# Last batch of a gated cross-attention layer with routed experts: tile loads issued one by one, and routing steps placed in other slots of the vector engine's program

## The reference, cut to what matters

```python
x = x + tanh(g_xattn) * xattn(layernorm(x), ctx, mask, Wq, bq, Wk, bk, Wv, bv, Wo, bo)  # 16 heads, causal
x = x + tanh(g_ffn)  * ffn(layernorm(x), W1, b1, W2, b2, Wr, br)                        # 8 experts

def ffn(x):
    pick = argmax(softmax(x @ Wr + br))            # one expert per token
    out = 0
    for i in range(8):
        xi = x * (pick == i)                       # rows of other tokens are zero
        out = out + (relu(xi @ W1[i] + b1[i]) @ W2[i] + b2[i])
    return out
```

## Time and profile before

| | us |
|---|---|
| median of 3 runs | 373.57 |
| lowest, highest run | 372.77, 375.61 |
| the profiled execution, own time | 377.75 |
| its span, first to last instruction | 376.0 |
| mean granted TensorE clock of the span | 0.986 of full speed |

### The profile page before, as it was taken

One profiled execution on the slowest core, in us unless ns is written; L12 is line 12 of the kernel. 1 busy time (PEld: TensorE's weight loads), 2 busy tenths in 40 slices (PEclk: granted clock), 3 DMA queues, 4 the chain that ended last, 5 costly groups with the idle time before them and its releaser, 6 DMA issues.

```text
span 376.0 us, 11155 instructions
## 1 busy us (share of the span) xinstructions
PE 352.0 (94%) x2825; PEld 283.4 (75%) x2825; DVE 272.5 (72%) x1278; ACT 256.2 (68%) x931; POOL 191.6 (51%) x369
## 2 busy tenths in 40 slices
PE   7999998999999999999999999999998966968992
PEld 5777777777877887787788777877785645858992
DVE  4789993889488858776785788497837786566762
ACT  3687794878688859866876787678755445645661
POOL 6155563476356733782477257636653450335554
PEclk9999999999999999999999999999999898999998
DMA  6997220002000300030003000300008505023320
GB/s 206 255 367 195 90 89 0 3 3 89 29 0 0 101 14 0 0 115 0 0 0 115 0 0 7 123 0 0 0 28 347 217 30 155 24 83 96 102 69 12
DMA packets 21562, 27.87 MB, mean 74 GB/s; under 512 B 3649, under 2 KB 16789, under 8 KB 21536
## 3 DMA queue, kind: packets, MB, share of 16 engines
q1 hardware_dynamic: 19776, 23.85, 20.0%
q0 software_dynamic: 1504, 3.16, 2.5%
q10 hardware_dynamic: 256, 0.56, 0.7%
HBM read 19.00 MB, written 9.01 MB: 74 GB/s over the span
## 4 chain that ended last, share of the span: by engine, by line
PE 80%; DVE 6%; issue 4%; DMA 3%; ACT 2%; POOL 2%; SPq 1%; another core or an unknown queue 1%; POOLq 0%; DVEq 0%; ACTq 0%
PE ps_kv L1221 15%; PE ps_o L1221 14%; PE ps_s L1221 13%; PE ps_t L1320 12%; PE ps_w L1221 10%; PE ps_q L1221 7%; PE ps_t L1221 6%; DMA tile_in<-sorted_rows 2%; DVE masked L787 1%; POOL out L503 1%; DVE prob_T L806 1%; ACT prob L561 1%; SPq L355 1%; DMA nat<-in_ctx 1%; PE ps_w L1352 1%
## 5 line engine op out<-in xcount | busy, mean ns | idle before, releaser
L432 POOL TENSOR_SCALAR prob<-prob,row_inv 128x128 f32<-128x128 f32 (+1 forms) x256 | 104.8, 430 | 131.2 <-DVE row_inv L800 131.0
L561 ACT ACTIVATE prob<-masked,neg_max 128x128 f32<-128x128 f32 (+1 forms) x256 | 113.4, 444 | 52.9 <-DVE neg_max L787 51.3
L787 DVE CUSTOM_DVE_ANT_0 masked<-ps_s,mask_now 128x128 f32<-128x128 f32 (+1 forms) x256 | 78.9, 353 | 57.3 <-PE ps_s L1221 54.8
L806 DVE COPY prob_T<-ps_t 128x384 f32<-128x384 f32 x128 | 67.3, 548 | 1.4 <-PE ps_t L1320 1.4
L1320 PE MATMUL ps_t<-ident,prob 128*128 128x128 f32 x384 | 57.2, 284 | 3.2 <-DVE prob_T L806 3.0
L1320 PEld LDWEIGHTS ps_t<-ident,prob 128*128 128x128 f32 x384 | 41.4, 142 | 24.8 <-issue 20.8
L1221 PE MATMUL ps_s<-k_T,q_T 64*128 64x128 f32 (+1 forms) x512 | 59.6, 351 | 0.0
L1221 PE MATMUL ps_o<-prob_T,v_nat 128*64 128x256 f32 (+1 forms) x512 | 56.4, 342 | 0.0
L561 ACT ACTIVATION_READ_ACCUMULATOR prob<-masked,neg_max 128x1 f32 x256 | 47.8, 187 | 0.0
L1221 PEld LDWEIGHTS ps_o<-prob_T,v_nat 128*64 128x64 f32 x512 | 31.4, 137 | 17.4 <-issue 3.0
L503 POOL DMA_INDIRECT out<-tile_out,tile_in x23 | 23.7, 1031 | 37.2 <-DVE tile_out L1170 23.3
(11 more groups left out here) (197 smaller groups left out, 546.5 us busy)
## 6 DMA issues: line engine op xcount, KB each, us to landing
ctx_buf<-in_ctx SPq DMA_DIRECT2D x8, 768.0 KB
sorted_rows<-pad_rows SPq DMA_DIRECT2D x8, 642.5 KB
tile_in<-sorted_rows SPq DMA_DIRECT2D x24, 128.5 KB
packs<-in_L_ffn_W SPq DMA_DIRECT2D x1, 2048.0 KB
packs<-in_L_ffn_W SPq DMA_DIRECT2D x8, 256.0 KB
nat<-in_ctx SPq DMA_DIRECT2D x8, 128.0 KB, 3.6
nat<-in_x SPq DMA_DIRECT2D x1, 768.0 KB, 6.5
w_in<-in_L_xattn_Wk SPq DMA_DIRECT2D x2, 256.0 KB, 4.5
```

Source lines behind the costliest of these rows:

```text
L432: g.tensor_scalar(prob[:, slot, lo:hi], prob[:, slot, lo:hi], row_inv[:, slot, t:t + 1], 1.0, ALU.mult, ALU.mult).then_inc(prob_ready, 1)
L561: s.activation(prob[:, slot, lo:hi], masked[:, slot % 2, lo:hi], ACT.Exp, bias=neg_max[:, slot, t:t + 1], scale=-1.0, accum_out=row_sum[:, ...
L787: v.tensor_tensor_reduce(out=masked[:, slot % 2, lo:hi], in0=ps_s[slot % 2][:, lo:hi], in1=mask_now[:, lo:hi], scale=-SCALE, scalar=FLOOR, ...
L806: v.tensor_copy(prob_T[:, slot % TSLOTS, :], ps_t[slot % 2][:, 0:W3]).then_inc(probT_kept, 1)
```

## The change

SP reads the place of each early tile just before it issues that tile's load; the waits for the padding and for the scattered rows stand between the first read and the first load. On DVE, in the last batch: the 16 steps of the second norm stand in slots 0 to 7 in place of 0 to 9; the empty rows in slot 10 in place of 23; rest in slot 16 in place of 29; the early table in slots 28 and 30 in place of 24 to 27. On PE the transposes of the normalised rows stand in step 2 ahead of the values, in place of the end of step 1, and `rest_product` directly behind them in place of step 4. On ACT rest's store stands in step 3 in place of 5, its broadcast load in step 4 in place of 6; the first five `early_w1` stay in steps 5 and 6.

```diff
             sp.wait_ge(early_table_ready, 1)
-            early_at = [sp.value_load(tile_row[0:1, k:k + 1], min_val=0, max_val=PADROW) for k in range(EARLY)]
-            sp.wait_ge(padded, 16 * (E + 1))
-            sp.wait_ge(scattered, 16 * (NT - QT))
             for k in range(EARLY):
-                sp.dma_start(tile_in[:, k], sorted_rows[bass.ds(early_at[k], P), :]).then_inc(tile_loaded[k], 16)
+                at = sp.value_load(tile_row[0:1, k:k + 1], min_val=0, max_val=PADROW)
+                if k == 0:
+                    sp.wait_ge(padded, 16 * (E + 1))
+                    sp.wait_ge(scattered, 16 * (NT - QT))
+                sp.dma_start(tile_in[:, k], sorted_rows[bass.ds(at, P), :]).then_inc(tile_loaded[k], 16)
...
                     keep_oT(b, 8 * b + j, j)
-                    if last and j == REST_AT + 1:
+                    if last and j == 3:
                         act.wait_ge(rest_ready, 1)
                         act.dma_start(rest_rows[:, :], rest[:, :]).then_inc(rest_stored, 16)
+                    if last and j == 4:
+                        act.wait_ge(rest_stored, 16)
+                        act.dma_start(rest_all[:, :, :], rest_rows.rearrange("e d -> (e d)").partition_broadcast(P)
+                                      ).then_inc(rest_loaded, 16)
+                    if last and j == 5:
                         act.wait_ge(early_table_ready, 1)
                         act.wait_ge(ld_ffn, 16 * (E + 2))
                         for tile in range(2):
                             early_w1(tile)
-                    if last and j == REST_AT + 2:
-                        act.wait_ge(rest_stored, 16)
-                        act.dma_start(rest_all[:, :, :], rest_rows.rearrange("e d -> (e d)").partition_broadcast(P)
-                                      ).then_inc(rest_loaded, 16)
+                    if last and j == 6:
                         for tile in range(2, 5):
                             early_w1(tile)
...
-                if here == 6 * REST_AT - 1:
+                if here == EMPTY_AT:
                     dve.wait_ge(empty_done, 1)
...
-                if here == 6 * REST_AT + 5:
+                if here == REST_AT:
                     dve.wait_ge(rest_done, 1)
...
-                        if j == REST_AT:
+                        if j == 2:
+                            norm_transposes(b - 1, b + 1)
                             rest_product()
                     values(p, j)
                     if last and j > 0:
                         last_projection(j - 1)
-                    if last and j == 1:
-                        norm_transposes(b - 1, b + 1)
...
-REST_AT = 4
-LAST_NORM = {0: (0,), 1: (1,), 2: (2, 3), 3: (4, 5), 4: (6, 7), 5: (8, 9), 6: (10, 11), 7: (12, 13), 8: (14,), 9: (15,)}
+EMPTY_AT, REST_AT = 10, 16
+LAST_NORM = {0: (0,), 1: (1, 2, 3), 2: (4, 5), 3: (6, 7), 4: (8, 9), 5: (10, 11), 6: (12, 13), 7: (14, 15)}
 LAST_CHOOSE = {17: (0, 1, 2, 3, 4, 5)}
 LAST_PLACE = {21: (0, 1), 22: (2, 3)}
-LAST_TABLE = {24: (0, 1), 25: (2, 3), 26: (4, 5), 27: (6, 7)}
+LAST_TABLE = {28: (0, 1, 2, 3), 30: (4, 5, 6, 7)}
```

## The result

The changed kernel takes 369.77 us (median of 9 runs, 369.55 to 371.34) against 374.28 us before (median of 9, 372.77 to 377.04): a ratio of 0.9886, interval 0.9854 to 0.9919. It is 4.5 us faster (3.0 to 5.5 by the interval); the forecast said 4.4 and a time of 369.2. Times after also lie closer together: 1.8 us from lowest to highest, against 4.3.

A forecast was written before the change was run, and what follows sets the result against it. PE is busiest (94%), but DVE was taken to bound the last batch's stretch. Filled idle time and earlier table and loads bring batch 7's transposes 4.5 us earlier, less a tenth: 373.57 - 4.4 = 369.2 us, range 367.0 to 372.4.

The forecast's parts named there:

- The sum: Whole change: batch 7's transposes 4.5 us earlier, a tenth lost, saving 4.4 us carried whole to the end.
- Step 6: Batch 7's transposes: PE's order and DVE's norm both arrive near 318.1, 4.5 us earlier than 322.62.
- Step 5: SP's early tile loads: first load at 305.6, 4.6 us earlier; only 0.5 to 2.5 reach PE.
- Step 2: Table in slots 28 and 30: table 1.3 us earlier, PE's 2.44 wait shrinks, about 2 us gap before pair 7's transposes.
- Step 4: ACT: pair 7's output copied at 310.3, not 312.86; rest's store and broadcast cost nothing.
- Step 1: Norm, empty and rest rows on DVE and PE: filled idle time brings pair 6's copies 1.8 us earlier, to 304.8.
- Rival B: PE's low clock after two waits goes, gaining another 1.5 to 2 us: 367.4 us; chance 0.12.
- Rival C: The low clock moves to the new gap at 303.3, costing some 8 us, 1.5 hidden: 375.7 us; chance 0.06.

The follow-up runs named there:

- moves-only run: The changed kernel with SP's old seven reads put back ahead of the first load; ratio to before 0.9896.
- after again: The changed kernel, unaltered, timed and profiled a second time; 370.5 us, ratio to before 0.9866.
- later weight copies: The changed kernel with the last three of DVE's seven weight copies behind batch 7's choice and late table; ratios to before 0.9843 and, run again, 0.9833.
- one-filler profile: The kernel before plus 20 identity transposes, never read, on PE where it waited for tile 0; ratio to before 1.0001.
- norm and rest only: The kernel before with the moves of norm, empty and rest rows, but the old table slots and SP reads; ratio to before 0.9942.
- SP's edit alone: The kernel before with only each early tile's place read just before its load; ratio to before 0.9952.
- before again: The kernel before, unaltered, timed and profiled a second time; 375.45 us, ratio to before 0.9992.
- table only: The kernel before with only the early table moved to slots 28 and 30; ratio to before 1.001.
- two fillers: The kernel before plus never-read identity transposes on PE, 12 ahead of the norm's transposes and 20 ahead of tile 0; ratio to before 0.9982.

## Why the prediction was right, point by point

*The sum* was 4.4 and the measured medians differ by 4.5. That they agree to a tenth is in part luck: the sum was made of rows of a profile with both low stretches, where the transposes gained 5.1 us and the end 6.9, and the interval of the measured gain is 3.0 to 5.5. Its times of day against the profile after: copies of pair 6 at 304.8, measured 304.56; the table 304.8, measured 304.5; norm at 313.4, measured 312.95; transposes at 318.1, measured 317.49. PE's first product was put at 311.6 and came at 310.65. Tile 0's load was to go 4 to 5 us earlier and went 3.6 earlier.

*Step 6, both sides meet near 318.* Right in form: PE and DVE arrive within 0.84 us of each other, and DVE's seven weight copies are what ends last. This was shown by the moves-only run, by after again, and by the later weight copies, which gave 1.0.

*Step 5, SP's reads.* The load was to go at 305.6, or 0.6 later for the scatter; it went at 306.60, 1.0 later, for the scatter. It landed in 2.0 to 2.2 us as taken. That the edit would no longer be on the path was right, but "0.5 to 2.5 of it reach PE" was the wrong measure: 0.7 reaches the first product, none the transposes. Reads between loads did not slow down, 268 ns and not the bound of 747. The floor of about 600 ns, which the Trainium skill gives for such a read in "DMA: Bandwidth & Descriptors", section "Latency and other measured facts", is not met by these reads: a read with what follows it takes 0.55 us, the load instruction itself 0.27. Only the reads of `pad_at`, with a median of 747 ns, are above it.

*Step 2* foresaw the new gap ahead of pair 7's transposes (305.4, measured 305.27; the wait was 1.54 us). *Step 4* was too dear by 0.7 us (pair 7's output copied at 309.59, not 310.3): the idle time ahead of ACT's three weight copies fell from 0.57 to 0.17, and pair 6's output came 0.2 earlier.

*Step 1 is the term whose cause was taken wrongly.* I put DVE's idle times of 1.42 and 1.64 us down to the order of the program, and "1.8 earlier" to filling them. The one-filler profile has the same order at full clock, with its table read 1.5 us earlier; against that, the changed kernel reads the table only 0.2 us earlier (23.2 to 23.0): the norm's moves give 0.7 (22.5 in norm and rest only), the later slots take 0.5 of it back. The copies of pair 6, for which the 1.8 was worked out, stand at 25.3 from the batch's start in the profiled before, at 23.7 with one filler and at 23.1 in the changed kernel. So against the profiled before 1.8 was near enough (2.2 measured), but 1.6 of it are a low clock that no longer comes, and 0.6 are the order's. Without any low clock the transposes move from 38.37 to 36.0, 2.4 us; against the profiled before, with its two low stretches, from 41.3, 5.3 us. The median gain of 4.5 lies between the two. The times bear this out: 371.9 to 372.0 us for the filler kernel's three executions at the higher clock, against 369.55 to 369.77 for the lowest five of the nine of the changed kernel (clock 0.990 to 0.994), 2.3 us. The one execution of SP's edit alone with a mean clock of 0.998 took 369.80, hardly more than those. Rival B was thus inside my own sum, and I counted it as a case beside it.

*The 6.9 us of the two spans*, counted from the batch's start 7.1: 5.3 up to the transposes; 0.7 from there to tile 7's load, where DVE waited 1.61 us for the ranks in the profiled before and 0.50 in the changed kernel and in before again; and 1.1 behind tile 7's load. The last is not this change's: that stretch takes between 40.5 and 43.1 us in the profiles with an unchanged tail, the lowest in SP's edit only. The granted clock over this stretch is 0.98 in the shortest and 0.89 in the two longest, but 0.96 in the profiled before with its 42.8: the clock seems a part of it, and what else moves it stays open. I expected the saving to arrive unaltered at the end; whether it does, the medians cannot tell, since the median execution's gain at the transposes is not known.

*Rival C*, that the low clock moves, happened as a mechanism in four kernels (table only, two fillers, norm and rest only, and once in the changed kernel), each time at the gap near pair 6 or 7. It never reached the price that I gave it, 8 us less 1.5: it was worth some 2 us at most at the transposes (norm and rest only), and nothing where DVE ends last. The rule that the Trainium skill has in "TensorE: Matmul & The Clock Gate", section "What's actually happening", that low is the default state and activity releases it, agrees with low stretches behind waits; which waits are followed by one it did not tell here.

## What to carry to other kernels

Before counting an idle time as the program's, look at the granted clock of the stretch, and at a second profile of the same program: here half of the gain at the transposes was a low clock that came behind a wait of PE in four profiles of five. Edits that each shorten one of several paths into the same point need not add up: SP's edit brought the transposes forward by 2.6 us alone and not at all beside the moves, and the table's move gained no time alone. And when work is put off to bring one point forward, look at what frees the buffers behind it: 2 us won at tile 7's load were given back by two stores put off.

## What the runs showed of the hardware that was not expected

The low level of TensorE's clock does not follow from the wait ahead of it alone. In the last batch a wait of 1.74 us was followed by windows of 0.5 to 0.7 in four profiles and by 1.00 in one, of the same program up to there; a wait of 2.44 us by 1.00 in four and by 0.50 in one; one of 2.35 us by 1.00; one of 1.54 us, in the changed kernel and its variants, by 1.00 in six and by 0.75 in one. At the low level a group of eight matmuls took 1.54 us in place of 0.87. Every low stretch in the batch began in the last part of a wait of at least 1.5 us or within 1.3 us behind its end.
